# Gates of two up-projection batches moved from TensorE to VectorE, and half of z's blocks loaded by SyncE

## The reference, cut to what matters

```
z = layernorm(x1)                                  # (4, 512, 1024)
logits = z @ gate_w                                # (4, 512, 8)
r = sum of the two largest logits of a row         # top_k(logits, 2), summed
h = relu(z @ up_w) ** 2                            # (4, 512, 2048)
shared = h @ down_w
routed = (((z @ fc1_w) @ expert_w) * r) @ fc2_w
out = x1 + layernorm(shared + routed) * gamma + beta
```

## Time and profile before

| what | value |
|---|---|
| median of 3 executions | 2096.97 us (2096.8 to 2096.99) |
| profiled execution | 2096.07 us, its span 2094.3 us |
| PE busy | 2075.6 us, 99% |
| DVE busy | 803.4 us, 38% |
| ACT busy | 694.6 us, 33% |
| POOL busy | 752.9 us, 36% |
| DMA | 286.31 MB, 137 GB/s in the mean |

### The profile page before, as it was taken

The page is one execution under the profiler, slowest core; times in us unless marked ns, Lnnn a source line. Parts: engine busy times, 40 slices in busy tenths (PEclk is TensorE's granted clock), DMA queues, the critical chain, the costliest instruction groups (busy, mean ns, idle before and its releaser), DMA issues.

```text
span 2094.3 us, 30295 instructions
## 1 busy us (share of the span) xinstructions
PE 2075.6 (99%) x9580; PEld 1732.6 (83%) x9580; DVE 803.4 (38%) x1419; ACT 694.6 (33%) x1209; POOL 752.9 (36%) x616
## 2 busy tenths in 40 slices
PE   8999999999999999999999999999999999999998
PEld 7888888888888888888888878787878888888887
DVE  4221312178888888831121412313231232222222
ACT  5121111167777777741111223112123311111111
POOL 2533030147777777662222343010024322222221
PEclk9999999999999999999999999999999999999999
DMA  6743433535655655534347555253433622222222
GB/s 197 258 166 140 152 119 110 180 83 147 156 149 151 161 152 141 130 115 151 128 159 200 195 162 155 105 150 111 133 97 134 211 87 89 90 88 82 77 82 76
DMA packets 302751, 286.31 MB, mean 137 GB/s; under 512 B 146896, under 2 KB 214480, under 8 KB 301776
## 3 DMA queue, kind: packets, MB, share of 16 engines
q1 hardware_dynamic: 188128, 196.58, 30.0%
q10 hardware_dynamic: 114544, 88.76, 14.9%
HBM read 184.32 MB, written 100.68 MB: 136 GB/s over the span
## 4 chain that ended last, share of the span: by engine, by line
PE 97%; DVE 1%; ACT 1%; DMA 0%; issue 0%; POOL 0%; DVEq 0%; POOLq 0%; ACTq 0%
PE psum L118 30%; PE psum L119 30%; PE psum L120 30%; PE psum L985 3%; PE psum L1031 1%; PE psum L1032 1%; PE psum L1012 1%; PE psum L1013 1%; PE psum L1697 0%; PE psum L1696 0%; DMA staging<-in_wqkv 0%; DVE operands L353 0%; PE psum L232 0%; DVE small L181 0%; DMA staging<-in_ctx 0%
## 5 line engine op out<-in xcount | busy, mean ns | idle before, releaser
L118 PE MATMUL psum<-operands 128*128 128x512 f32 (+3 forms) x2904 | 1115.8, 384 | 10.3 <-DVE operands L353 9.8
L119 PE MATMUL psum<-operands 128*128 128x512 f32 (+3 forms) x2904 | 1113.8, 384 | 0.0
L120 PE MATMUL psum<-operands 128*128 128x512 f32 (+3 forms) x2904 | 1111.0, 383 | 0.0
L118 PEld LDWEIGHTS psum<-operands 128*128 128x128 f32 (+1 forms) x2904 | 546.6, 188 | 109.7 <-DVE operands L353 9.5
L120 PEld LDWEIGHTS psum<-operands 128*128 128x128 f32 (+1 forms) x2904 | 547.0, 188 | 105.5
L119 PEld LDWEIGHTS psum<-operands 128*128 128x128 f32 (+1 forms) x2904 | 547.5, 189 | 94.1
L1276 POOL TENSOR_TENSOR operands<-staging,operands 128x512 fp32r<-128x512 f32 x92 | 118.5, 1300 | 348.7 <-ACT operands L1271 348.3
L1157 DVE TENSOR_REDUCE small<-psum 128x1 fp32r<-128x576 f32 x256 | 192.9, 754 | 89.9 <-PE psum L985 89.8
L1935 POOL TENSOR_TENSOR operands<-operands 128x640 fp32r<-128x640 f32 x64 | 100.2, 1566 | 319.8 <-ACT operands L1930 319.4
L905 POOL TENSOR_TENSOR operands<-staging,operands 128x512 fp32r<-128x512 f32 x128 | 164.4, 1292 | 34.8 <-ACT operands L1079 26.0
L1786 DVE TENSOR_TENSOR staging<-staging 128x512 f32<-128x512 f32 x64 | 46.5, 745 | 326.1 <-ACT staging L1744 325.3
(11 more groups left out here) (123 smaller groups left out, 1283.8 us busy)
## 6 DMA issues: line engine op xcount, KB each, us to landing
h_scratch<-staging ACTq DMA_DIRECT2D x80, 256.0 KB, 2.2
operands<-h_scratch SPq DMA_DIRECT2D x64, 320.0 KB, 3.1
operands<-recip_scratch SPq DMA_DIRECT2D x64, 192.0 KB, 4.5
o_scratch<-staging SPq DMA_DIRECT2D x64, 192.0 KB, 4.9
operands<-o_scratch SPq DMA_DIRECT2D x64, 192.0 KB, 2.8
operands<-q_hi_scratch ACTq DMA_DIRECT2D x14, 768.0 KB, 5.9
operands<-q_lo_scratch ACTq DMA_DIRECT2D x14, 768.0 KB, 6.0
staging<-in_x SPq DMA_DIRECT2D x20, 512.0 KB, 3.9
```

Of the source, the lines that this page charges most:

```text
L118: e.matmul(o, lh, rh, start=first, stop=False)
L119: e.matmul(o, lh, rl, start=False, stop=False)
L120: return e.matmul(o, ll, rh, start=False, stop=last)
```

## The change

In the bodies of batches 0 and 1 the gates stay on PE. Those of batches 2 and 3 are computed one batch earlier, in the bodies of batches 1 and 2, on VectorE: r needs the 8 logits of each row of z, and here each logit is the sum over 1024 products, in two halves. The gate weights come transposed (`gate_t`), are copied to a scratch in DRAM, and are loaded as 16 rows of 512 numbers, each spread over all 128 partitions, into two buffers that lie where the gate weights' parts were. For each row VectorE runs four `tensor_tensor_reduce` on 128x512 (one for each tile of 128 rows of z), which write their products into a spare bank and the sum into a small tile. Rows 0 to 3 come behind group 0's squares, 4 to 9 behind group 1's, 10 to 15 behind group 2's, with the chain that gives r behind them. With one bank each instruction waits for the end of the one in front (rows 0 to 3), with two for the one before that.

For this the normalized rows must be there earlier and stay longer: ACT issues x1's load at the body's start and z's store behind group 1; VectorE normalizes ahead of group 0's squares, and ACT's square root comes before group 0. The blocks may overwrite the rows only when the sums are done: ACT issues the first 16 behind group 3 and SP the other 16 at its body's end; both wait for the chain's first link. SP issues rows 0 to 11 ahead of f3's load and rows 12 to 15 ahead of f0's. VectorE's two middle bodies are written out instead of looped, and PE has two loops of two batches.

```diff
@@ -1649,11 +1650,51 @@
                 return (JOBS_FIRST, M_FIRST) if b == 0 else (JOBS_LAST, M_LAST)
             return JOBS_MID, b * N_MID + (M_MID - N_MID)
 
+
+        GR = 2 * NE
+        g_row = [MM[:, 22 * SLOT + r * NB:22 * SLOT + (r + 1) * NB] for r in range(2)]
+        g_acc = sm[:, 0:ST * GR].rearrange("p (t e) -> p t e", t=ST)
+        g_rl = [sem(f"gate_row_loaded{r}") for r in range(2)]
+        g_use = sem("gate_row_used", ST + 1)
+
+        def d_gate_row_in(e, b, i):
+
+            if i == 0:
+                e.wait_ge(*past(g_rl[0], 16))
+                e.sem_inc(idle, 1)
+                e.wait_ge(*past(d_gm, 2))
+                e.sem_inc(idle, 1)
+            e.wait_ge(*past(g_use, b * (ST * GR) + ST * (i - 1 - GR)))
+            e.sem_inc(idle, 1)
+            e.dma_start(raw(g_row[i % 2]), g_d[i * NB:(i + 1) * NB].partition_broadcast(P)).then_inc(g_rl[i % 2], 16)
+
+        def d_gate_row(e, b, i, banks):
+
+            x, h = i // 2, i % 2
+            n = ((b - 1) * GR + i) * ST
+            e.wait_ge(*past(g_rl[i % 2], 16 * ((b - 1) * NE + x) + (32 if h == 0 else 16)))
+            for t in range(ST):
+                e.wait_ge(*past(g_use, n + t + 1 - banks))
+                e.tensor_tensor_reduce(PS[:, 7 - (t + 1) % banks, :], XN2[:, t, h * NB:(h + 1) * NB], raw(g_row[i % 2]), 1.0, 0.0, ALU.mult, ALU.add,
+                                       g_acc[:, t, h * NE + x:h * NE + x + 1]).then_inc(g_use, 1)
+
         def d_sp_eng(e):
             for b in (0, None, B - 1):
                 def run(b, n_before):
                     for m, (at, j) in enumerate(flat(jobs_of(b)[0])):
+                        if not isinstance(b, int) and at == 3:
+                            for i in range(12):
+                                d_gate_row_in(e, b, i)
+                        if not isinstance(b, int) and at == 4:
+                            for i in range(12, GR):
+                                d_gate_row_in(e, b, i)
                         job_load(e, j, n_before + m)
+                    if not isinstance(b, int):
+                        e.wait_ge(*past(d_gc, b * GC + (GC + 1)))
+                        e.sem_inc(idle, 1)
+                        e.wait_ge(*past(d_zs, (b + 1) * 16 + 16))
+                        e.sem_inc(idle, 1)
+                        d_blocks_in(e, b + 1, 1)
 
                 if b is not None:
                     run(b, jobs_of(b)[1])
@@ -1674,7 +1715,7 @@
                         run(r, jobs_of(r)[1])
 
         def d_pe(e):
-            def body(b, last):
+            def body(b, gates):
                 def wait_bank(g, c):
                     if g == 0:
                         e.wait_ge(*past(d_ev, b * ND - 2 + c))
@@ -1701,12 +1742,13 @@
                         e.sem_inc(idle, 1)
                         e.transpose(PS[:, 6, 0:P], gTs, ident[:]).then_inc(d_gt, 1)
 
-                mm_groups(e, b, D_GROUPS, d_zl, wait_bank, job_slot, d_acc, slot_ready, gate, d_fr)
+                mm_groups(e, b, D_GROUPS, d_zl, wait_bank, job_slot, d_acc, slot_ready, gate if gates else None, d_fr)
 
             e.wait_ge(*past(cc_x1, B * ST - 1))
-            with e.Fori(0, B - 1) as b:
+            with e.Fori(0, 2) as b:
+                body(b, True)
+            with e.Fori(2, B) as b:
                 body(b, False)
-            body(B - 1, True)
 
         def d_act(e):
             def body(b, last, first=False):
@@ -1729,7 +1771,11 @@
                             d_rows_in(e, 1, 2 * m[0] if m[0] > 1 else 0, 2 * m[0] + 2)
                         m[0] += 1
 
+                if not last and not first:
+                    d_load(e, x1_d, b + 1)
                 run(-1, b)
+                if not last and not first:
+                    d_sqrt(e, b + 1)
                 n, sq = 0, 0
                 for g, chunks in enumerate(D_GROUPS):
                     if g == len(D_GROUPS) - 1 and not last:
@@ -1754,15 +1800,12 @@
                         row = ch[1] * P if up else F + ch[1] * P
                         e.dma_start(h_d[bass.ds(b * (F + L) + row, P), :], st2[c]).then_inc(d_st[c], 16)
                         n += 1
-                    if g == 0 and not last and not first:
-                        d_load(e, x1_d, b + 1)
-                    if g == 2 and not last and not first:
+                    if g == 1 and not last and not first:
                         d_z_out(e, b + 1)
-                    if g in (3, 4) and not last and not first:
-                        d_blocks_in(e, b + 1, g - 3)
                     run(g, b)
-                    if g == 1 and not last and not first:
-                        d_sqrt(e, b + 1)
+                    if g == 3 and not last and not first:
+                        e.wait_ge(*past(d_gc, b * GC + (GC + 1)))
+                        d_blocks_in(e, b + 1, 0)
 
             body(0, False, True)
             with e.Fori(1, B - 1) as b:
@@ -1772,6 +1815,10 @@
         def d_dve(e):
             def body(b, last, first=False):
                 n = 0
+                to_gate = not last and not first
+                if to_gate:
+                    d_norm(e, b + 1)
+                    e.wait_ge(*past(d_zn, b + 2))
                 for g, chunks in enumerate(D_GROUPS):
                     final = g == len(D_GROUPS) - 1 and not last
                     for k in range(2 if final else 0):
@@ -1787,31 +1834,35 @@
                         n += 1
                     if final:
                         d_lo(e, b + 1, DK - 1)
-                    if g == 0:
+                    if g == 0 and b < 2:
                         e.wait_ge(*past(d_gm, b + 1))
                         e.sem_inc(idle, 1)
                         for t in range(ST):
                             m = e.tensor_copy(gT[t], PS[0:2 * NE, 6, t * P:(t + 1) * P])
                         m.then_inc(d_gl, 1)
-                    if g == 1:
+                    def link(ins, b, q):
+                        ins.then_inc(d_gc, 1)
+                        e.wait_ge(*past(d_gc, b * GC + q))
+                        e.sem_inc(idle, 1)
+
+                    def top2(b, sums):
+                        link(e.tensor_tensor(g8, sums[:, :, 0:NE], sums[:, :, NE:2 * NE], ALU.add), b, 2)
+                        for t in range(ST):
+                            link(e.max(gtop[:, t, :], g8[:, t, :]), b, 3 + t)
+                        link(e.tensor_tensor(rw[:, b * ST:(b + 1) * ST], gtop[:, :, 0], gtop[:, :, 1], ALU.add), b, GC)
+
+                    if g == 1 and b < 2:
                         e.wait_ge(*past(d_gt, b + 1))
                         e.sem_inc(idle, 1)
-                        q = [0]
-
-                        def link(ins):
-                            q[0] += 1
-                            ins.then_inc(d_gc, 1)
-                            e.wait_ge(*past(d_gc, b * GC + q[0]))
-                            e.sem_inc(idle, 1)
-
-                        link(e.tensor_copy(gsum, PS[:, 6, 0:P].rearrange("p (t e) -> p t e", t=ST)[:, :, 0:2 * NE]))
-                        link(e.tensor_tensor(g8, gsum[:, :, 0:NE], gsum[:, :, NE:2 * NE], ALU.add))
-                        for t in range(ST):
-                            link(e.max(gtop[:, t, :], g8[:, t, :]))
-                        link(e.tensor_tensor(rw[:, bass.ds(b * ST, ST)], gtop[:, :, 0], gtop[:, :, 1], ALU.add))
-                        assert q[0] == GC
-                    if g == 1 and not last and not first:
-                        d_norm(e, b + 1)
+                        link(e.tensor_copy(gsum, PS[:, 6, 0:P].rearrange("p (t e) -> p t e", t=ST)[:, :, 0:2 * NE]), b, 1)
+                        top2(b, gsum)
+                    if to_gate and g < 4:
+                        for i in range((0, 4, 10, GR)[g], (4, 10, GR, GR)[g]):
+                            d_gate_row(e, b, i, 2 if g else 1)
+                    if to_gate and g == 2:
+                        e.wait_ge(*past(g_use, b * (ST * GR)))
+                        link(e.tensor_copy(gsum, g_acc), b + 1, 1)
+                        top2(b + 1, gsum)
 
             e.wait_ge(*past(d_gw, 16))
             e.tensor_copy(GW[:, :, 0:NE], graw).then_inc(d_gw, 1)
@@ -1821,7 +1872,7 @@
             e.memset(gTs, 0.0).then_inc(d_gw, 1)
             e.wait_ge(*past(d_gw, 19))
             body(0, False, True)
-            with e.Fori(1, B - 1) as b:
+            for b in range(1, B - 1):
                 body(b, False)
             body(B - 1, True)
 
...
+            e.dma_start(g_d, gate_t).then_inc(g_rl[0], 16)
+        "gate_t": np.asarray(inputs[_F + "gate_w"]).T.reshape(-1),
```

More of the change, by code:

```diff
@@ L3, with xattn_ffn_kernel @@
 from contextlib import ExitStack
-def xattn_ffn_kernel(nc, x, xt, ctx, wqkv, wo, gate_w, up_w, down_w, fc1_w, fc2_w, expert_w, gamma, beta, out):
+def xattn_ffn_kernel(nc, x, xt, ctx, wqkv, wo, gate_w, gate_t, up_w, down_w, fc1_w, fc2_w, expert_w, gamma, beta, out):
     f32 = mybir.dt.float32
@@ L54, in xattn_ffn_kernel @@
```

(3 more changed lines are left out.)

## The result

The changed kernel takes 2101.14 us (median of 22 runs, 2097.78 to 2104.0) against 2096.99 of the kernel before: a ratio of 1.002 with a 95% interval of 1.0014 to 1.0026, so 4 us slower. Forecast were 2091.2 and faster. The profiled execution took 2103.29, with a span of 2101.3: 7.0 above the span of before.

The account below looks back on a forecast made before the run. TensorE, busy 99% of the span, was taken as the bound: 7.8 us of gates removed less 2.0 of waits gives 5.8 faster, 2096.97 - 5.8 = 2091.2. Own range 2090 to 2094.5; the range leaving 2 in 10 out, 2089 to 2108.

Parts of the forecast that it names:

- What is taken away: On PE, batches 2 and 3 lose sixteen gate matmuls and a transpose each: 7.8 us, the most to be gained.
- Where it is late: VectorE's rows delay squares, ACT's split, blocks and group 4's evacuation; PE waits at its last group, g6.
- One instruction: VectorE's multiply-and-sum on 128x512: 0.68 us with two banks, 0.80 with one, the sum's write-out included.
- Rivals B and C: VectorE's multiply-and-sum: B, serial accumulator, 0.85 each, 2107.6, chance 0.18; C, half rate, 1.21 each, 2147, chance 0.06.
- the sum of the waits: At g6, rows take 51.6 us against budgets of 51.1 and 50.1; PE waits 0.5 in body 1, 1.5 in body 2.
- The start: x1's load lands in 8.0 us, normalization takes 10.7; rows start at 1337.5 in body 1, 1449.6 in body 2.
- The rows' loads: A 256 KB row load takes 3.0 us, 3.3 easily; beside z's store row 6 lands 5.9 behind its free buffer.
- POOL beside VectorE: POOL's contention on VectorE's SBUF reads is hidden in the 2.4 us wait before row 12.
- The blocks: ACT issues 16 block transfers in 8.6 us, between f3's split and group 4's evacuation.
- rival D: ACT's block issue is slowed by SP's, instruction as forecast: 2097 to 2101; chance 0.24 together with the middle cases.
- budgets: Time left for 16 rows on VectorE before PE waits at g6: 51.1 us in body 1, 50.1 in body 2.

Follow-up runs that it names:

- gates_off: The kernel before without PE's sixteen gate matmuls and transpose for batches 2 and 3, nothing in their place; 2088.04 us (0.9962).
- half_columns: The changed kernel with each multiply-and-sum on 256 of its 512 columns, half of each dot product left out; 2087.42 us (0.9958).
- after_again: The changed kernel, unchanged, run again for a second trace; 2097.32 us (span 2095.3).
- z_quarter: The changed kernel with only one of the four tiles of z stored in the middle bodies; 2092.41 us (0.9983).
- jobs_first: The changed kernel, but ACT splits f2 and f3 ahead of the stores that wait for the squares; 2103.7 us (1.0035).

## Why the prediction was wrong

*What is taken away*: right. gates_off gives 7.8.

*Where it is late*: right in the main. The chain rows, chain, squares, f3's split, ACT's blocks, group 4's evacuation, g6 is the one that PE waits on, and half_columns shows that the length of the rows in it decides. Missing was group 4 (below).

*One instruction*: 0.65 with two banks and 0.79 with one, for 0.68 and 0.80. The sum's write-out is an instruction of its own, as the Trainium skill has it (VectorE: DVE Perf Modes, Two Vector instructions with no wait between them), and costs 0.05 over the plain 0.60. Rivals B and C are out: neither a serial accumulator nor half rate. The Trainium skill (Vector Engine (DVE) Microarchitecture Reference, 7. Points that are easy to get wrong) states for `S2S2D2_STT` that two SBUF sources that are not bf16 halve the throughput. Here that does not show: with both f32 sources in SBUF the instruction starts every 0.65 us for 512 elements, and the measurement decides. The trace calls it CUSTOM_DVE_ANT_0; whether it is of the kind that the page means is not shown.

*The step that failed* is the sum of the waits. The step said 0.5 us in body 1 and 1.5 in body 2. In the two traces it was 3.3 and 2.3 in body 1, and 6.0 and 6.1 in body 2, of which 4.6 and 4.7 came at g6 and 1.5 at group 4. Taken from the first matmul of each body (1315.02 and 1432.78, and 1311.75 and 1426.92 in after_again), in us:

| stretch | body 1: forecast | body 1: two traces | body 2: forecast | body 2: two traces |
|---|---|---|---|---|
| body's start to the rows' start | 24.3 | 25.4, 25.4 | 23.7 | 23.9, 24.3 |
| first row to the end of the last (R) | 57.3 | 58.0, 57.5 | 55.0 | 58.3, 58.0 |
| R to g6 | 15.3 | 16.3, 15.9 | 15.3 | 16.4, 16.5 |
| less PE's own time to g6 | 96.4 | 96.4 | 92.5 | 92.5 |
| PE waits | 0.5 | 3.3, 2.3 | 1.5 | 6.1, 6.3 |

The forecasts follow from the prediction's dates, with body 1 beginning a group (16.3) ahead of its gates at 1329.5; the last row of the table also holds a few small spacings, so it is up to 0.2 above the gaps. Body 2's error is mostly the length of the rows (3.0 and 3.3 of 4.6 and 4.8). Body 1's is the rows' later start (1.1), the stretch behind the rows (1.0 and 0.6) and their length (0.7 and 0.2). The terms that were mis-sized:

- The start. x1 is asked for some 0.6 us later in the body than I took, and takes 8.5 to 9.2 instead of 8.0. The rows of body 1 start 1.1 later by it.
- The rows' loads. I took 5.9 us for a load beside z's store in both bodies. In body 1 that held, and rows 4 to 9 took 19.4 and 19.7 for 19.8. In body 2, where they begin just ahead of the store, it was up to 8.1, and VectorE waited 5.2 to 5.7 instead of 3.2. Rows 4 to 9: 21.9 and 22.1. z_quarter takes this away and gets 3.5 us back there.
- POOL beside VectorE. I held its contention to be hidden in the wait before row 12. It makes two instructions of rows 10 and 11 1.0 longer each, and row 12 still waits up to 1.8 behind them, as its load stands behind f3's, which waits for POOL's second half. Rows 10 to 15: 19.9 to 20.4 for 19.0.
- The blocks. The 16 take 9.5 to 10.2 on ACT instead of 8.6. In body 1 ACT's step is 0.54 from one to the next until SP issues its own beside them (from 1406.70 on), and then up to 0.95. This is a third of rival D: the 2101 lies at the upper end of D's numbers, but D's mechanism has only this part in it.

*Left out altogether*: that f2's slot hangs on the squares of group 2, which stand behind rows 4 to 9, so that lateness reaches PE at group 4 too (1.5 us in body 2; jobs_first and z_quarter remove it); and that TensorE pays for a long wait twice, once in the wait and once in slow matmuls behind it (1.0 in one trace, 2.8 in the other). After_again's 2.1 net comes without much of the latter. The two traces are 6.0 us apart in span: 1.7 of these lie in batch 0's gaps, 1.8 in slow matmuls, 0.9 in the gaps of bodies 1 and 2 and 1.1 ahead of the stage. What makes up the rest of the scatter from 2097.8 to 2104 no trace shows, and what makes batch 0's gaps stays open.

The forecast had the right place, but by its own sum the rows ended 0.5 and 1.5 us behind their budgets, so that every error in a load or an issue went straight onto PE. 2.0 of waits were forecast and 8.5 and 9.3 came in bodies 1 and 2, without the slow matmuls.

## What to carry to other kernels

When work is put on an idle engine, what stands behind it in that engine's queue matters more than the work: list every reader of the delayed results (here evacuation, a weight slot and the turns), with the time at which each wants it, and let short urgent things go ahead. A gain that depends on an order can be had by splitting the work around the urgent instruction and by taking DMA issues off the engine that also evacuates: the same gates, on the same engines, went from 4 us slower to 8 us faster so. And when loads are asked for one buffer ahead, count each big transfer beside them at its worst (here 8.1 us for a load that takes 3.0 to 3.4 otherwise).

## What the runs showed of the hardware

- A multiply-and-sum of two f32 tiles of 128x512 in SBUF with its product into PSUM starts every 0.65 us, or 0.79 where each waits for the end of the last; a POOL instruction that reads SBUF at the same time (1.3 alone, 1.5 to 1.9 then) makes one of them 1.77.
- Behind gaps of PE of 3.3 us and more in these traces (3.3, 4.6; 4.7; 3.7, 6.5; 4.3, 8.6) some matmuls started 0.427 apart at a granted clock of 0.50 to 0.57 in the stretch; behind those of up to 2.3 us (2.3; 1.1, 1.5, 2.2; 1.1, 1.9) none did. They cost 1.0 to 4.0 us per execution.
- 16 DMAs of 32x32 blocks take 8.6 us to issue on ACT alone and 9.4 to 11.6 beside SP's 16.
